# A Mamba-like block and an attention block on one core: nine taps of the last 64 channels as six TensorE products, z's and x's remainders in one tile, the norm's scale and shift folded into the weights

## The reference, cut to what matters

```
xn = layernorm over channels of x, times ln_w, plus ln_b      (192 channels)
xc, z = split(in_proj_w @ xn)                                 (192 + 192 channels)
xc = silu(depthwise 3x3 conv(xc) + conv_b)                    (one 3x3 filter per channel)
... four scans over xc, summed ...
y = layernorm(y) * silu(z);  x = x + out_proj_w @ y
... attention on x, residual added ...
```

## Time and profile before

| | |
|---|---|
| median of 3 runs | 10451.7 us |
| profiled execution, its own time | 10460.32 us |
| its span, first to last instruction | 10458.4 us |
| mean granted TensorE clock | 0.94 of full |
| PE busy | 9132.7 us (87%) |
| DVE busy | 7813.8 us (75%) |
| ACT busy | 6224.0 us (60%) |
| POOL busy | 3667.5 us (35%) |

### The profile page before, as it was taken

How to read it: one execution, slowest core, us unless ns; L and a number is a source line. 1 busy time by engine, 2 the same in 40 slices (tenths; PEclk the granted TensorE clock), 3 DMA queues, 4 the chain that set the end, 5 groups by cost and what they waited for, 6 DMA issues and landing times.

```text
span 10458.4 us, 108398 instructions
## 1 busy us (share of the span) xinstructions
PE 9132.7 (87%) x27904; PEld 4899.5 (47%) x27904; DVE 7813.8 (75%) x9039; ACT 6224.0 (60%) x7683; POOL 3667.5 (35%) x1920
## 2 busy tenths in 40 slices
PE   5999959999599995999959999699996999969999
PEld 2336723367233662336623366233662336623366
DVE  6977669866698666976669776697666976669776
ACT  4755647556475554755557555575555755557555
POOL 3850038500385003850048500485004850048500
PEclk8999979999799997999979999799997999979999
DMA  1320013200132001320013200132001320013200
GB/s 43 109 71 5 8 38 109 72 5 8 40 108 72 5 8 44 105 70 5 8 44 109 66 7 6 44 109 67 6 6 44 110 67 5 7 45 109 67 5 8
DMA packets 158736, 487.41 MB, mean 47 GB/s; under 512 B 21177, under 2 KB 21785, under 8 KB 125486
## 3 DMA queue, kind: packets, MB, share of 16 engines
q1 hardware_dynamic: 158254, 482.04, 14.6%
HBM read 454.69 MB, written 27.26 MB: 46 GB/s over the span
## 4 chain that ended last, share of the span: by engine, by line
PE 59%; issue 16%; DVE 15%; POOL 4%; ACT 3%; DVEq 1%; DMA 0%; ACTq 0%; SPq 0%; POOLq 0%
DVE h L1039 6%; PE ps L509 5%; PE ps L522 5%; PE ps L510 5%; PE ps L524 5%; PE ps L523 5%; PE ps L511 5%; PE ps L432 4%; PE ps L355 3%; PE ps L393 2%; PE ps L390 2%; PE ps L377 2%; PE ps L374 2%; PE ps L347 2%; PE ps L348 2%
## 5 line engine op out<-in xcount | busy, mean ns | idle before, releaser
L1164 DVE TENSOR_TENSOR pl<-pf,ph 128x1024 fp32r<-128x1024 f32 x1024 | 1254.7, 1225 | 1205.2 <-ACT ph L823 1204.1
L1039 DVE TENSOR_TENSOR_SCAN h<-ps,h,dbu 128x512 f32<-128x512 f32 x1536 | 1884.4, 1268 | 17.7 <-DVE h L1065 5.2
L897 POOL TENSOR_TENSOR dbu<-bs,du 128x1024 f32<-128x1024 f32 x768 | 1799.8, 2373 | 52.8 <-POOL du L888 52.8
L823 ACT ACTIVATE ph<-pf 128x1024 fp32r<-128x1024 f32 x1024 | 1085.3, 1060 | 833.5 <-PE ps L524 833.3
L842 POOL MEMSET xb<- 64x1024 f32 x16 | 15.2, 947 | 4280.2 <-issue 4276.5
L815 ACT ACTIVATE pf<-ps 128x1024 f32<-128x1024 f32 x1024 | 1051.0, 1026 | 644.6 <-PE ps L511 644.6
L697 ACT ACTIVATE ps<-dt,negA 128x512 f32<-128x512 f32 x1536 | 1032.6, 683 | 440.4 <-DVE h L1039 406.3
L1148 DVE TENSOR_REDUCE mx<-ps 128x1 f32<-128x512 f32 x1792 | 1164.8, 683 | 68.7 <-PE ps L432 42.2
L1047 DVE TENSOR_TENSOR hc<-h,ps 128x1024 f32<-128x1024 f32 x768 | 937.8, 1221 | 194.3 <-PE ps L366 114.5
L888 POOL TENSOR_TENSOR du<-dt,u 128x512 f32<-128x512 f32 x512 | 707.5, 1404 | 625.8 <-DVE dt L1029 625.8
L522 PE MATMUL ps<-ph,gth 128*97 128x512 f32 x2048 | 817.7, 399 | 80.8 <-ACT yraw L803 72.1
(11 more groups left out here) (175 smaller groups left out, 15899.1 us busy)
## 6 DMA issues: line engine op xcount, KB each, us to landing
bs<-rows SPq DMA_DIRECT2D x256, 1024.0 KB, 5.1
bs<-rows SPq DMA_DIRECT2D x512, 256.0 KB, 6.1
xa<-in_x SPq DMA_DIRECT2D x128, 256.0 KB, 2.9
xb<-in_x SPq DMA_DIRECT2D x128, 128.0 KB, 3.0
out<-fa SPq DMA_DIRECT2D x64, 256.0 KB, 2.0
out<-fa SPq DMA_DIRECT2D x64, 128.0 KB, 2.3
rows<-xd SPq DMA_DIRECT2D x256, 8.0 KB
gate<-in_sel SPq DMA_DIRECT2D x1, 384.0 KB
```

The source lines that it names most:

```text
L823: A(ph[:, mp % 2, :, :], pf[:, mp % 2, :, :], ACT.Copy).then_inc(S["ph_ready"], 1)
L897: pool.tensor_tensor(dbu[:, q, :, :], bs[par][:, q, :, :], du[:, r:r + 1, :].to_broadcast([P, 2, T]), ALU.mult).then_inc(S["dbu_ready"], 1)
L1039: dve.tensor_tensor_scan(h[:, j, ::step], ps[:, 2 + e, ::step], dbu[:, q, e, ::step], h[:, j, end:end + 1], ALU.mult, ALU.add)\
L1164: TT(pl[:, mp % 2, :, :], pf[:, mp % 2, :, :], ph[:, mp % 2, :, :].bitcast(F32), ALU.subtract)\
```

## The change

Four things are done, in the project stage and around it.

1. **Taps.** The first 128 channels stay on DVE: 8 instructions a chunk, each now waiting for the one before it (they all add into the same tile). The last 64 channels go to PE. `pad1` holds the remainder in partitions 0 to 63 and the same image shifted by one column in 64 to 127, so one product with a weight matrix `tapw` (tap values on two diagonals, built by POOL for each image) applies two taps; six products give all nine, the centre included. They write PSUM bank 5, and ACT copies it with the bias to `u`.
2. **One tile for both remainders.** z's and x's 64 remaining channels are one product pair: the projection is 6 products and not 8.
3. **The norm.** The weights are multiplied by ln_w once, and ln_b's contribution is a row of the weights against the row of ones. DVE's multiplication by 1/deviation writes `na`, `nb` directly.
4. **The image's boundary.** The next image's first two chunks are loaded during the attend stage, `xa`, `xb` and `fa` have memory of their own, SP does not wait for its outputs before the barrier, and `xb`'s zeros are set earlier.

The diff, cut to its core:

```diff
+        for j in range(6):                                     # PE: remainder(c)
+            src = padi[1][:, bass.ds(c * RPC + j // 2, RPC), 2 * (j % 2):2 * (j % 2) + WW]
+            m = mm(flat(ps[:, 5, :]), tapw[:, j, :], src, start=(j == 0), stop=(j == 5))
+        m.then_inc(S["rem_ready"], 1)
...
                         pe.wait_ge(S["norm_ready"], i * 2 + 4)
                         pe.wait_ge(S["gate_ready"], i + 1)
-                        two(4, 2)
-                        two(5, 3).then_inc(S["z_ready"], 1)
+                        pe.wait_ge(S["tap_ready"], i + 1)
+                        two(3, 2)
+                        two(4, 1).then_inc(S["z_ready"], 1)
+                        two(2, 0).then_inc(S["xc_ready"], 1)
...
-                    if "p" in which:
-                        pe.wait_ge(S["tap_ready"], i * 2 + 2)
-                        two(2, 0)
-                        two(3, 1).then_inc(S["xc_ready"], 1)
+                    if "c" in which:
+                        last = isinstance(c, int) and c > NCH
+                        pe.wait_ge(S["tap_ready"], (b * NCH + (c - 2 if last else c - 1)) + 2)
+                        remainder(c - 2)
...
+                    if "u" in which:                           # ACT, first in its step
+                        act.wait_ge(S["rem_ready"], w + 1)
+                        A(u[:, 1, bass.ds((c - 3) * T, T)], ps[:, 5, :], ACT.Identity, bias=vecs[:, V_CB + 1:V_CB + 2])\
+                            .then_inc(S["rem_free"], 1)
...
-                        for r in range(2):
-                            A(padi[r][:, bass.ds(c * RPC + 1, RPC), 1:1 + WW], flat(ps[:, 2 + r, :]), ACT.Copy)
+                        A(padi[0][:, bass.ds(c * RPC + 1, RPC), 1:1 + WW], flat(ps[:, 2, :]), ACT.Copy)
                         for r in range(2):
-                            A(u[:, r, bass.ds(c * T, T)], ps[:, 2 + r, :], ACT.Identity,
+                            A(padi[1][r * R:r * R + R, bass.ds(c * RPC + 1, RPC), 1 - r:1 - r + WW], flat(ps[R:P, 4, :]), ACT.Copy)
+                        A(u[:, 0, bass.ds(c * T, T)], ps[:, 2, :], ACT.Identity, bias=vecs[:, V_CB:V_CB + 1],
...
-                        TT(da[:, :], da[:, :], rstd[:, :], ALU.mult).then_inc(S["scaled"], 1)
-                        TT(db[:, :], db[:, :], rstd[0:R, :], ALU.mult).then_inc(S["scaled"], 1)
+                        TT(na[:, :], da[:, :], rstd[:, :], ALU.mult).then_inc(S["norm_ready"], 1)
+                        TT(nb_[0:R, :], db[:, :], rstd[0:R, :], ALU.mult).then_inc(S["norm_ready"], 1)
...
-                        pool.tensor_scalar(na[:, :], da[:, :], vecs[:, V_LNW:V_LNW + 1], vecs[:, V_LNB:V_LNB + 1],
-                                           ALU.mult, ALU.add).then_inc(S["norm_ready"], 1)
-                        pool.tensor_scalar(nb_[0:R, :], db[:, :], vecs[0:R, V_LNW + 1:V_LNW + 2],
...
+                for q in range(2):                             # SP, attend stage, ahead of the outputs
+                    load((b + 1) % nb, (b * 2 + 2) * NCH + q, q, q)
...
-                sp.wait_ge(S["out_stored"], b * (32 * NCH) + (32 * NCH + 32))
```

More of the change, by code:

```diff
@@ L115, in build @@
         mx = sb("mx", [P, 4, NU // 4], where=vx)
+        xa = sb("xa", [P, 2, T], where=vx)
+        xb = sb("xb", [P, 2, T], where=vx)
+        fa = sb("fa", [P, 2, T], where=vx)
         lnx = ExitStack()
-        xa = sb("xa", [P, 2, T], where=lnx)
-        xb = sb("xb", [P, 2, T], where=lnx)
         da = sb("da", [P, T], where=lnx)
@@ L133, in build @@
         cs = sb("cs", [P, 2, T], where=lnx)
+        tapw = sb("tapw", [P, 6, P], where=lnx)
         lnx.close()
@@ L265, in _, with load @@
             barrier(sp, 0, -1)
-            with sp.Fori(0, nb) as b:
[L267 to L276, removed]
+            def load(im, i, c, q):
+                sp.wait_ge(S["x_free"], i + 1)
+                sl = bass.ds(c * T, T)
+                sp.dma_start(xa[:, q, :], xr[im, 0:P, sl]).then_inc(S[f"x_loaded{q}"], 16)
+                sp.dma_start(xb[0:R, q, :], xr[im, P:C, sl]).then_inc(S[f"x_loaded{q}"], 16)
+            for q in range(2):
+                load(0, q, q, q)
+            with sp.Fori(0, nb) as b:
+                sp.wait_ge(S["out_stored"], b * (32 * NCH) + 32)
+                sp.sem_inc(mark, 1)
+                with sp.Fori(1, NCH // 2) as cc:
+                    for q in range(2):
+                        load(b, (b * 2) * NCH + cc * 2 + q, cc * 2 + q, q)
                 barrier(sp, b, 0)
@@ L290, in _ @@
                 barrier(sp, b, 1)
-                loads(1)
+                with sp.Fori(0, NCH // 2) as cc:
+                    for q in range(2):
+                        load(b, (b * 2 + 1) * NCH + cc * 2 + q, cc * 2 + q, q)
                 barrier(sp, b, 2)
+                for q in range(2):
+                    load((b + 1) % nb, (b * 2 + 2) * NCH + q, q, q)
                 with sp.Fori(0, NCH) as c:
@@ L297, in _ @@
                     sp.dma_start(outr[b, P:C, sl], fa[0:R, 1, :]).then_inc(S["out_stored"], 16)
-                sp.wait_ge(S["out_stored"], b * (32 * NCH) + (32 * NCH + 32))
                 barrier(sp, b, 3)
+            sp.wait_ge(S["out_stored"], nb * (32 * NCH) + 32)
+            for q in range(2):
+                sp.wait_ge(S[f"x_loaded{q}"], nb * (32 * NCH) + 32)
         @block.tensor
@@ L304, in _ @@
             mm = pe.matmul
+            pe.wait_ge(s_load, NL)
+            mm(ps[0:1, 0, 0:3 * P], vecs[:, V_LNB:V_LNB + 1], win0[:, :], start=True, stop=False)
+            mm(ps[0:1, 0, 0:3 * P], vecs[0:R, V_LNB + 1:V_LNB + 2], win1[0:R, :], start=False, stop=True).then_inc(S["bias_row"], 1)
             barrier(pe, 0, -1)
@@ L323, in step @@
                         pe.wait_ge(S[f"x_loaded{q}"], (b * 2) * (16 * NCH) + (c + 1 - q) * 16 + 32)
+                        if isinstance(c, int) and c < 0:
+                            pe.wait_ge(S["xb_zero"], b + 1)
+                            pe.sem_inc(mark, 1)
                         mean_of(0, xa[:, q, :], xb[:, q, :], "mean_ready")
@@ L605, in _ @@
             A(negA[:, :], negA[:, :], ACT.Exp).then_inc(S["consts_set"], 1)
+            act.wait_ge(S["bias_row"], 1)
+            A(win1[R:R + 1, :], ps[0:1, 0, 0:3 * P], ACT.Copy)
             barrier(act, 0, -1)
@@ L641, in step @@
                         act.wait_ge(S["gate_ready"], i + 1)
-                        sigmoid(zs[:, :, :], ps[:, 4:6, :], "zs_ready", i * 3)
+                        sigmoid(zs[:, :, :], ps[:, 3:5, :], "zs_ready", i * 3)
                     if "n" in which:
@@ L837, in _ @@
             pool.memset(eps[:, :], 1e-5)
+            pool.memset(xb[:, :, :], 0.0).then_inc(S["xb_zero"], 1)
             barrier(pool, 0, -1)
@@ L849, in _ @@
             with pool.Fori(0, nb) as b:
-                zero_rows(b * 8 + 3, b * 2 + 1, (xb[R:P, :, :], sqb[R:P, :], nb_[R:P, :]))
-                for t in padi:
-                    for edge in (t[:, 0:1, :], t[:, PW - 1:PW, :], t[:, 1:PW - 1, 0:1], t[:, 1:PW - 1, PW - 1:PW]):
+                zero_rows(b * 6 + 2, b * 2 + 1, (sqb[R:P, :], nb_[R:P, :]))
+                for r, t in enumerate(padi):
+                    for edge in (t[:, 0:1, :], t[:, PW - 1:PW, :], t[:, 1:PW - 1, 0:1], t[:, 1:PW - 1, PW - 1 - r:PW]):
                         m = pool.memset(edge, 0.0)
                         m.then_inc(S["borders_set"], 1)
+                pool.memset(tapw[:, :, :], 0.0).then_inc(S["tapw_ready"], 1)
+                pool.wait_ge(S["tapw_ready"], b * 19 + 1)
+                pool.sem_inc(mark, 1)
+                for j in range(6):
+                    for r in range(1 + (j % 2 == 0)):
+                        rows_ = slice(r * R, r * R + R)
+                        t = V_TAP + 9 + 3 * (j // 2) + 2 * (j % 2) + r
+                        for half in range(2):
+                            pool.tensor_scalar(tapw[rows_, j, half * R:half * R + R], foldw[rows_, R:P], vecs[rows_, t:t + 1],
+                                               None, ALU.mult).then_inc(S["tapw_ready"], 1)
                 def step(c, par, which):
-                    j = b * NCH + (c + 1)
                     if "u" in which:
@@ L958, in deviate, with convolve @@
                     TT(db[:, :], srcb, ps[0:R, 0, :], ALU.subtract).then_inc(S["dev_ready"], 1)
-                FIRST_TAPS = 7
-                def convolve(c, part):
+                def convolve(c):
                     w = b * NCH + c
-                    for n in (range(FIRST_TAPS), range(FIRST_TAPS, 8))[part]:
+                    acc = chunk(u[:, 0], c, 0)
+                    for n in range(8):
                         t = n if n < 4 else n + 1
                         dy, dx = t // 3, t % 3
[L968 to L974, removed]
+                        src = padi[0][:, bass.ds(c * RPC + dy, RPC), dx:dx + WW]
+                        if n > 0:
+                            dve.wait_ge(S["conv_link"], w * 7 + n)
```

(2 more changed lines are left out.)

69 lines of the change are left out of this document (40 added, 29 removed).

## The result

The changed kernel takes 10094.5 us (median of 4 runs, 10089.66 to 10098.62) against 10451.5: ratio 0.9658, 95% interval 0.9641 to 0.9675. The forecast was 10090. The profiled execution took 10092.67 with a span of 10090.8, 367.6 us less than before.

What follows compares the result with a forecast made beforehand. DVE's 16 taps and POOL's norm behind them were taken to set the project step. Gains of 306 (stage), 53 (boundary) and 8 (memset), less 4 once per program, made 363 us: forecast 10090 us, range 10030 to 10195.

Steps and rivals of the forecast that it cites:

- What bounded before: Project stage: DVE's 16 taps and POOL's norm behind them set the full step of 17.7 us.
- The new step, 13.7: Project stage, full step: PE becomes the bound with 16 products of 0.86 us, 13.7 us in place of 17.7.
- The loop behind it: Full step: gate, deviation, squares, two sigmoids, logarithm and exponential, norm; with handoffs 13.4 us, only 0.3 below PE.
- The bound for a chained tap: DVE's taps, each waiting for the one before: between 0.74 and 0.86 us, taken as 0.78.
- The clock: Steps 0 and 1: PE's idle time could bring half clock, up to 1.7 us added to each, taken as 0.9.
- The tail: End of the project stage: 32.2 us, or 35.6 if chained taps give POOL no gap; taken as 34.
- The boundary: Last output's issue to next image's first product: 8.4 us falls to a barrier of about 0.7; 53 us in all.
- A: Rival: PE still starts each project-stage step at half clock, 80 us more, 10170 us; chance 0.10.
- D: Rival: z's projection waits for ACT's centre tap and keeps the step at 17 us, 10220 us; chance 0.03.
- B: Rival: PE's tap products read slowly, like columns, a step of 18.9 us, 10370 us; chance 0.06.
- C: Rival: PE at half clock throughout, a step of 27.4 us, slower at 10840 us; chance 0.02.
- The last step of the sum: From profiled execution to median of the runs: 10097 us less 8.6, so 10089, forecast as 10090 us.

Runs made afterwards that it cites:

- foldonly: The kernel before with only the folded norm: DVE writes the normalized tiles, taps, tiles and boundary as before; 10306.9 us, ratio 0.9858.
- unroll: The changed kernel with the loop over the 8 images written out on every engine; 10018.1 us, ratio 0.9588.
- udve: The changed kernel with u times its sigmoid done by DVE instead of POOL; 10071.2 us, ratio 0.9633.
- fill: The changed kernel with two spare products behind the mean in steps 1 and 2, where PE otherwise idles; 10087.1 us, ratio 0.9645.

## Why the prediction was right, and where its terms were not

- **What bounded before**: right. foldonly gives DVE's own step of 16.85 once POOL's norm is out of the way, inside the 16.4 to 16.8 that the rows gave but for 0.05.
- **The new step, 13.7**: right, 13.73, and PE is busy throughout. The loop behind it was put at 13.4 and is 13.1 to 13.2. The bound for a chained tap (0.74 to 0.86) holds only in the steps that are written out, 0.79 from start to start (6.26 for eight). In the rolled loop, for which 0.86 was meant, it is 0.89 to 0.92, and eight taps with POOL's product between them take 8.91, at the far end of the 8.3 to 9.0. It cost nothing, since PE sets those steps.
- **The clock**: right in its place and size. In each of the 8 images exactly one of steps 0 and 1 takes 12.8 instead of 11.1, 1.7 us; the forecast had 0.9 for each. Chunk 2's projection came 36.3 after the first product (forecast 36.2) and chunk 7's 104.6 (104.5).
- **The tail, taken as 34 between 32.2 and 35.6**: it is 32.0 in the first image, the lower value. The chained taps leave POOL its gap, and POOL is never shut out. That made the new stage some 2 us an image too long (138.5 against a mean of 136.7). The other 0.9 an image by which the term was short is that I had used the first image's 176.7 for all, whose mean is 177.6. The second window of the earlier trace rows was given the length of the first; that image's stage took 178.2.
- **The boundary, 7.6 for each of 7 images**: the step that was mis-sized. It took for granted that only a barrier of 0.7 would remain. The pause fell from 8.6 to 5.4 us, 3.2 each; unroll shows what stayed, the jump back: without it the pause is 1.2. It was there in the trace of before: POOL's first memset followed SP's first load by 2.7 us, although both stood behind the same barrier and nothing else held the memset. SP's own jump takes 0.3 us in that trace, those of the other four engines 2.6 to 4.4. The two rows, from the timeline of before:

```profile
1324.78 0.37 SPq L274 DMA_DIRECT2D xa<-in_x  x1
...
1327.45 0.95 POOL L842 MEMSET xb<- 64x1024 f32 x1 [611.74 <-issue]
```

- **The scan, not forecast**: 17 us. In the first image it is 3.8 us shorter, and 1.7 of that is gone before its first chunk. In before the clock was still at half 4.5 us after the scan's first product, in after no longer:

```profile
202.69 2.07 PE L347 MATMUL ps<-u,wx 128*128 128x512 f32 x2 [34.16 <-POOLq L174]
...
207.22 3.66 PE L355 MATMUL ps<-xd,wdt 128*128 128x512 f32 x4 [0.76 <-ACT xd L664]
```

```profile
164.99 2.07 PE L384 MATMUL ps<-u,wx 128*128 128x512 f32 x2 [8.92 <-POOLq L176]
...
169.47 1.98 PE L392 MATMUL ps<-xd,wdt 128*128 128x512 f32 x4 [0.76 <-ACT xd L709]
```

  PE had idled 34 us before the first and 8.9 before the second; but the pause is not the cause: scans of the changed kernel with the same 8.9 take from 497.4 to 500.7 us, and in foldonly PE idles 36 us ahead of a first scan that takes 497.3. Between the short scans and the long ones lie products at half clock in two short stretches (1.06 us for what takes 0.59), in the second chunk and near the scan's end. What decides where they fall stays open, and so how much of the 17 us the change brought.
- **The rivals**: A and D fall with the step of 13.73, B with tap products 0.86 apart, C with a granted clock of 1.00.

That the total came within 5 us is luck to the extent of these terms: +21 and +17 against -30 and -5. The last step of the sum was off as well: the profiled execution took 4 us less than the forecast's 10097, but the median of the runs lies 1.8 above it and not 8.6 below.

## What to carry to other kernels

When a bound moves from one engine to another, write down the loop behind the new bound as well: here 13.7 and some 13.2 lay so close that taking 2.6 us of work off PE gained 0.5. Cut the ends of a pipelined stage out of the sum and work them out by themselves, since work that is hidden in the steps can stand in a queue there: before, one of the two instructions of POOL's norm took 11.4 us there in place of 0.8, and its product 9.5 in place of 2.3. Before a pause at a loop's end is booked as gain, compare when two engines behind the same barrier start: what differs is the price of the jump.

## What the runs showed of the hardware that I had not expected

- The jump back to the head of the image loop costs each engine of the changed kernel 3.3 to 4.7 us with no wait shown (in the kernel before SP's takes 0.3; why is not shown). Written out, the pause at the boundary is 1.2 us in place of 5.0 to 6.1, and the scan stage gets 5.5 us shorter as well.
- In the kernel before, eleven taps, each 0.66 us after the last, ran before POOL's product got through, which so took 9.45 us. In the changed kernel, where each tap waits for the one before (0.79 us apart), POOL got in after one of them, at 1.96 us to DVE. The chain's longer distance between taps is the likely reason; no run changes it alone.
- An idle time of 2.31 us ahead of a projection brought the half clock in one of two like places in every image of the changed kernel. In udve, with the same two pauses, it was one of them in six images, both in one and neither in another; with pauses of 0.59 us (fill) it was never seen there.
